# A fused cross-attention and FFN kernel on one core: new orders of the setup's steps, of four early slots on GpSimd, of one batch's tiles and of N's high and low parts

## The chip, the core and the metric

The kernel runs on one core of a Trainium2 chip. The metric is the device time of one launch in microseconds. Three runs of the kernel before took 2051.66 us (median), from 2050.03 to 2053.55.

The engines are called PE or TensorE (matmuls), DVE or VectorE, ACT or ScalarE, POOL or GpSimd, and SP (it issues all transfers). Each engine takes its own list of instructions strictly in order and meets the others through semaphores: a wait in the middle of a list holds everything behind it on that engine.

## The reference

```
x = x + xattn(ctx, layernorm(x), fside, fside, ln1, ln2, Wq, Wkv, Wout)   # q scaled and shifted per head
x = x + tanh(layernorm(x) @ W.T @ aux1 @ aux2 + bias)

xattn:  ln = layernorm(latents);  kn = layernorm(context)
        q  = ln @ Wq (16 heads of 64);  k, v = kn @ Wkv
        q  = q * (1 + scale) + shift
        out = softmax(q k / 8) v;  out @ Wout
```

x is 16 batches of 1024 rows of 512; the context has 64 rows in each batch. All is float32 at full accuracy, so every operand of a product is split into a high and a low part and each product is made of three matmuls (high by high, high by low, low by high).

## The kernel before, in words

**What is precomputed.** The three FFN matrices are multiplied into one, W3. For each batch the queries never appear: M (512 x 1024) is Wq times that batch's keys, so that the scores of a tile of 128 rows are x M, and N (1024 x 512) is that batch's values times Wout, so that the attention's output is p N.

**The setup** (`setup_sp`, `setup_pool`, `setup_act`, `setup_dve`, `setup_pe`, to about 133 us) loads 22 chunks of weights through a ring of five buffers, and eight tiles of context through three. Each engine runs a list of steps. The step `split c` of a chunk is ACT's high part (L419, or L411 and L415 where the columns are centred), then a low part by DVE (L476, L471) or, for the chunks in `POOL_LO`, by POOL (L373); SP loads chunk c + 5 into the buffer once chunk c is split. `stats i` and `norm i` (L449 to L453, POOL's pow at L367, L458, L462) normalise context tile i. `turn i` is its four transposes (PE L590), ACT's high part (L424) and DVE's low part (L482) in N_hi and N_lo, which serve as buffers here. `kv n` (32 of them, four buffers in PSUM) is one product of context and weights: sixteen of v (n under 16; ACT copies it out at L428), sixteen of k (DVE scales it twice in `k_scale`, L525 and L527), stored by SP at L312 from two buffers `kv_out`. `kb` sums the bias (PE L534, L535; ACT's copy at L385; SP's store at L287). Products kv 0 to 7 need turns 0 to 3, and kv 8 to 15 need turns 4 to 7 with their low parts. PE's order stands in `pe_steps`; before, SP, ACT, DVE and POOL share one list behind their front lists, `later_steps`, made from `beside`.

**Then M of batches 0 and 1** is made in 16 steps (`fold_m_pe`, L757 to L759; `m0_act` L768, `m0_dve` L783, and the copies of batch 1's part at L763 into eight buffers `m1_raw`, which SP stores at L347). The first four buffers lie in `stage_more`, the next two in two x buffers, the last two in the buffer S of the scores.

**The slots.** 128 tiles of rows go through a pipeline, one tile a slot: slot t computes the scores of tile t (PE, 24 matmuls), the product p N of tile t-2 (24), W3 of tile t-4 (12). m is t mod 8; a batch has eight tiles. For a tile, DVE adds the bias to the scores (L1319) and takes maxima (L1324), POOL subtracts them (L1458), ACT takes exp (L1222), DVE sums (L1330, L1333), POOL normalises (L1465), SP writes p and reads it back rearranged (L1067, L1084), DVE turns it (L1341), ACT and DVE make its high and low parts pT_hi and pT_lo (L1227, L1350). The next tile's xT_hi and xT_lo are ACT's and POOL's (L1020, L1025).

**N of the next batch** is made in the slots with m = 1 from the second batch on (t = 9, 17, ..., 121): `fold_n_pe` makes eight products of three matmuls at the slot's end (bank<-Wo_hi,bdv). Four banks hold them, so product p from the fifth on waits for the low part of product p-4:

```python
                if p < len(use):
                    free(p)
                else:
                    pe.wait_ge(s_nl, b8 + p - len(use) + 1)
```

ACT copies each to N_hi (L981), DVE subtracts for N_lo (L987). In `slot_act` and `slot_dve` this stands at the slot's end, behind the first half of the previous tile's p:

```python
            if tile_of(t - 1):
                pT_hi_part(0, t - 1)
            ...
            if m == 1 and 1 < t < T:
                fold_n_act(act, t - 1, range(8))
```

The next slot's scores wait for the fifth and sixth low part, since they use the same banks.

**M of the batches from 2 on** is made beside the slots in 128 small tiles (`tile_pe`, L877 to L880), four places A to D in a slot, given by `tile_at`: batches 2 and 3 (32 tiles of two batches, where DVE adds two halves, L891) in slots 2 to 9, four in each; batches 4 to 7 in slots 10 to 25, two in each; batches 8 to 15 in slots 26 to 89, one in each. Even ones of the first 32 use bank 2, which the fold of N uses too. They are stored, and loaded again a batch ahead as `land` (L942), split by ACT (L957) and POOL (L961).

Of the kernel before, what the change touches and what calls it, by code (L numbers as in the profile page):

```python
# [1587 lines left out]
```

## Time and profile before

| | |
|---|---|
| median of three runs | 2051.66 us (2050.03 to 2053.55) |
| the profiled execution | 2051.34 us, of which the span from first to last instruction is 2049.5 |
| PE busy | 2027.4 us of the span, 99% |
| DVE, ACT, POOL busy | 1520.5, 1319.4, 1349.7 us |
| mean granted TensorE clock | 0.999 |
| DMA | 431.54 MB, 210 GB/s of it to and from HBM |

A row of a timeline gives the start in us from the span's start, how long it lasted, the engine, the line, the operation, output<-inputs, shapes and the number of instructions merged; in brackets, how long the engine was idle before it and what ended that. Matmuls overlap in the pipeline: one of 512 columns is shown 0.39 us long, but in a full stream they start 0.227 apart. DMA issues (SPq) are times of the queue, not of the transfer.

### The profile page before, as it was taken

How to read it: one execution, taken by the hardware profiler on the slowest of the kernel's cores; microseconds unless marked ns; L12 is line 12 of the kernel's file. 1: busy time of each engine (PE TensorE's matmuls, PEld its weight loads, DVE VectorE, ACT ScalarE, POOL GpSimd, SP SyncE). 2: the span in 40 equal slices, each digit the busy share in tenths (PEclk: the TensorE clock that was granted, in tenths of full speed). 3: DMA queues.
4: the chain of work that ended last, by engine and by line, in shares of the span. 5: the costliest groups of instructions: out<-in, count | busy, mean ns of one | idle time of the engine just before them, and what ended most of it. 6: DMA issues, size and time to landing. Idle time of an engine off the chain costs nothing.

```text
span 2049.5 us, 31380 instructions
## 1 busy us (share of the span) xinstructions
PE 2027.4 (99%) x9180; PEld 1681.4 (82%) x9180; DVE 1520.5 (74%) x2414; ACT 1319.4 (64%) x3005; POOL 1349.7 (66%) x1466
## 2 busy tenths in 40 slices
PE   9999999999999999999999999999999999999998
PEld 7777878888888888888888888888888888888887
DVE  7567777776777777777777777777777777787776
ACT  4455667666766666666666667666666666666654
POOL 3136766766676776767676776767677676767564
PEclk9999999999999999999999999999999999999999
DMA  7657988878787887878788787878767576666653
GB/s 263 197 176 211 271 232 245 251 225 248 222 227 206 219 223 208 226 204 231 195 232 219 208 224 206 230 197 217 211 185 211 174 207 179 200 184 191 178 170 118
DMA packets 502490, 431.54 MB, mean 211 GB/s; under 512 B 54832, under 2 KB 408240, under 8 KB 502320
## 3 DMA queue, kind: packets, MB, share of 16 engines
q1 hardware_dynamic: 502320, 429.54, 74.6%
q8 instruction: 74, 1.21, 0.3%
q14 instruction: 96, 0.79, 0.1%
HBM read 251.33 MB, written 178.06 MB: 210 GB/s over the span
## 4 chain that ended last, share of the span: by engine, by line
PE 86%; DVE 3%; DMA 2%; ACT 2%; issue 2%; POOL 2%; SPq 2%; DVEq 0%; ACTq 0%; POOLq 0%
PE bank L161 34%; PE bank L1176 21%; PE bank L166 17%; PE bank L1179 10%; DMA m_scratch<-evac 1%; PE bank L880 1%; PE bank L879 1%; POOL area L1458 1%; POOL area L1465 1%; DVE N_lo L987 0%; DVE area L1319 0%; SPq L321 0%; DVE row_max L1324 0%; DVE turned L1341 0%; ACT bank L992 0%
## 5 line engine op out<-in xcount | busy, mean ns | idle before, releaser
L1458 POOL TENSOR_TENSOR area<-area,row_max 128x256 f32<-128x256 f32 x512 | 353.8, 712 | 145.8 <-DVE row_max L1324 145.8
L1176 PE MATMUL bank<-N_hi,pT_hi 128*128 128x512 f32 x1024 | 398.7, 389 | 2.6 <-DVE N_lo L987 1.3
L161 PE MATMUL bank<-M_hi,xT_hi 128*128 128x512 f32 x1024 | 398.7, 389 | 0.0
L161 PE MATMUL bank<-M_lo,xT_hi 128*128 128x512 f32 x1024 | 398.7, 389 | 0.0
L1176 PE MATMUL bank<-N_lo,pT_hi 128*128 128x512 f32 x1024 | 398.6, 389 | 0.0
L1227 ACT CAST pT_hi<-turned 128x512 fp32r<-128x512 f32 x256 | 159.1, 622 | 337.4 <-DVE turned L1341 337.4
L1465 POOL TENSOR_TENSOR area<-area,row_inv 128x512 f32<-128x512 f32 x256 | 269.2, 1052 | 114.7 <-DVE row_inv L1333 114.6
L1482 POOL TENSOR_TENSOR area<-area 128x512 f32<-128x512 f32 x127 | 165.4, 1303 | 239.3 <-ACT area L1266 239.3
L1330 DVE TENSOR_REDUCE row_sum<-area 128x8 f32<-128x512 f32 x256 | 174.4, 681 | 167.5 <-ACT area L1222 166.7
L1350 DVE TENSOR_TENSOR pT_lo<-turned,pT_hi 128x512 fp32r<-128x512 f32 x256 | 196.1, 766 | 119.2 <-ACT pT_hi L1227 119.2
L166 PE MATMUL bank<-M_hi,xT_lo 128*128 128x512 f32 x1024 | 273.9, 389 | 0.8 <-POOL xT_lo L1025 0.7
L1179 PE MATMUL bank<-N_hi,pT_lo 128*128 128x512 f32 x1024 | 273.7, 389 | 0.0
L1222 ACT ACTIVATE area<-area 128x512 f32<-128x512 f32 x256 | 160.2, 626 | 127.8 <-POOL area L1458 127.1
L1176 PEld LDWEIGHTS bank<-N_hi,pT_hi 128*128 128x128 f32 x1024 | 192.2, 188 | 42.3 <-DVE N_lo L987 1.5
L166 PEld LDWEIGHTS bank<-M_hi,xT_lo 128*128 128x128 f32 x1024 | 192.1, 188 | 41.4 <-POOL xT_lo L1025 1.7
L1179 PEld LDWEIGHTS bank<-N_hi,pT_lo 128*128 128x128 f32 x1024 | 192.2, 188 | 39.9
L1176 PEld LDWEIGHTS bank<-N_lo,pT_hi 128*128 128x128 f32 x1024 | 192.3, 188 | 39.5
L161 PEld LDWEIGHTS bank<-M_lo,xT_hi 128*128 128x128 f32 x1024 | 192.3, 188 | 39.4
L161 PEld LDWEIGHTS bank<-M_hi,xT_hi 128*128 128x128 f32 x1024 | 192.3, 188 | 39.4 <-ACT xT_hi L1020 0.2
L1319 DVE SCALAR_TENSOR_TENSOR area<-bank,rs,area 128x512 f32<-128x512 f32 x256 | 187.1, 731 | 19.7 <-PE bank L166 15.9
L161 PE MATMUL bank<-W_lo,x2T_hi 128*128 128x512 f32 (+1 forms) x512 | 199.3, 390 | 0.0
L161 PE MATMUL bank<-W_hi,x2T_hi 128*128 128x512 f32 (+1 forms) x512 | 199.0, 389 | 0.0
(183 smaller groups left out, 3923.3 us busy)
## 6 DMA issues: line engine op xcount, KB each, us to landing
p_scratch<-area SPq DMA_DIRECT2D x256, 256.0 KB, 2.6
p_moved<-p_scratch SPq DMA_DIRECT2D x512, 128.0 KB, 4.3
area<-x_dram SPq DMA_DIRECT2D x128, 256.0 KB, 4.5
area<-x_turned_dram SPq DMA_DIRECT2D x128, 256.0 KB, 4.0
x_scratch<-area SPq DMA_DIRECT2D x127, 256.0 KB, 3.0
x_moved<-x_scratch SPq DMA_DIRECT2D x508, 64.0 KB, 3.5
y_dram<-area SPq DMA_DIRECT2D x127, 256.0 KB, 3.6
land<-m_scratch SPq DMA_DIRECT2D x120, 256.0 KB, 2.8
```

What stands on the lines that cost most here:

```text
L161: mm = eng.matmul(ps, sh, mv, start=(n == 0), stop=False)
L166: mm = eng.matmul(ps, sl, mh, start=False, stop=(k == len(pairs) - 1))
L1176: pe.matmul(O_ps[:], st(pT_hi, k), n_cols(mv, k), start=(k == 0 and mv is N_hi), stop=False)
L1179: mm = pe.matmul(O_ps[:], st(pT_lo, k), n_cols(N_hi, k), start=False, stop=(k == 7))
L1222: act.activation(s, s, ACT.Exp).then_inc(s_ex[q], 1)
L1227: act.copy(half_of(pT_hi, q), turned[:]).then_inc(s_pTh[q], 1)
L1319: dve.scalar_tensor_tensor(out=half_of(S[t % 2], q), in0=S_ps[q][:], scalar=rs1[:, 0:1], in1=half_of(bias, q), op0=ALU.mult, op1=ALU.add). ...
L1330: dve.tensor_reduce(row_sum[t % 2][:, hs], heads(half_of(S[t % 2], q)), AX_XY, ALU.add).then_inc(s_sum[q], 1)
L1350: dve.tensor_tensor(half_of(pT_lo, q), turned[:], half_of(pT_hi, q).bitcast(F32), ALU.subtract).then_inc(s_pTl[q], 1)
L1458: last = pool.tensor_tensor(s, s, row.to_broadcast([P, 2, 4, J2]), ALU.subtract)
L1465: pool.tensor_tensor(s, s, inv, ALU.mult).then_inc(s_p[q], 1)
L1482: pool.tensor_tensor(xr[u % RING], xr[u % RING], hid, ALU.add).then_inc(s_y, 1)
```

## The change

1. The setup's shared list is cut into one for each engine. PE takes turn 3 ahead of the last part of W3, and turns 4 to 7 behind kv 2, 4, 5, 6 (before: 1, 3, 4, 5). DVE makes W3's low parts in the order 2, 3, 0, 1, with context tile 4's norm between, and takes stats, norm and turn of tiles 5 to 7 in a new order. ACT takes turns 4 to 7 behind kv 3, 5, 6, 7 (before 2, 4, 5, 6). The low parts of chunks 11 and 13 go from DVE to POOL. SP loads chunks 15 to 18 behind kv 2, 4, 6, 8 (before 0, 1, 4, 7), and context tile 7 behind kv 3 (before 1).
2. DVE's low parts of the four Wout chunks move one step later than ACT's high parts, and its k0 steps too. SP's first loads of x go from step 29 to 27.
3. The first high part of x moves from ACT to POOL.
4. M of batch 1 is staged first in S, then in the x buffers, then in `stage_more`; who needs S or the x buffers waits for the first four stores alone.
5. Slots 0 and 3 on POOL: the first subtraction goes ahead of xT_lo in slot 0, and xT_lo ahead of the two normalisations in slot 3.
6. The last four tiles of two batches go from slot 9 to slot 10, and all later tiles one slot on.
7. In the slots with m = 1, ACT makes N_hi 0 and 1 before pT_hi, and 2 to 7 after it. DVE makes N_lo 0 and 1 before the turn of p, N_lo 2 between the turn and pT_lo, and 3 to 7 after it.

```diff
-        m1_raw = [stage_more[...] for i in range(4)] + xr[2:4] + [S[0][...] for i in range(2)]
+        M1_EARLY = 4
+        m1_raw = [S[0][...] for i in range(2)] + xr[2:4] + [stage_more[...] for i in range(4)]
...
-                    ("w3_hi", 2), ("w3_lo", 2), ("turn", 2), ("w3_hi", 3), ("w3_lo", 3), ("turn", 3)]
+                    ("w3_hi", 2), ("w3_lo", 2), ("turn", 2), ("w3_hi", 3), ("turn", 3), ("w3_lo", 3)]
+        W3_LO = (2, 3, 0, 1)
...
-            some("turn", 2, 3) + some("split", 7, 8) + some("w3", 0, 1, 2, 3) + [("stats", 4), ("norm", 4)]
-        pool_front = some("stats", 0, 1) + some("split", 6) + some("stats", 2, 3) + some("split", 9) + some("stats", 4)
-        beside = {0: [("split", 10), ("stats", 5), ("norm", 5)], 1: [("split", 11), ("load", 7), ("stats", 6), ("norm", 6)],
-                  2: [("turn", 4), ("stats", 7), ("norm", 7)], 4: [("turn", 5), ("split", 12)],
-                  5: [("turn", 6)], 6: [("turn", 7)], 7: [("split", 13)],
-                  24: [("k0_load", 0)], 26: [("k0", 0)], 27: [("k0", 1)], 29: [("x0", 0)]}
+            some("turn", 2, 3) + some("split", 7, 8) + some("w3", *W3_LO[:2]) + [("stats", 4), ("norm", 4)] + some("w3", *W3_LO[2:]) + \
+            [("stats", 5), ("norm", 5), ("turn", 4), ("split", 10), ("stats", 6), ("norm", 6), ("turn", 5), ("stats", 7), ("norm", 7)] + \
+            some("turn", 6) + some("split", 12) + some("turn", 7)
+        pool_front = some("stats", 0, 1) + some("split", 6) + some("stats", 2, 3) + some("split", 9) + some("stats", 4, 5, 6) + \
+            some("split", 11) + some("stats", 7) + some("split", 13)
+        beside_sp = {2: some("split", 10), 3: some("load", 7), 4: some("split", 11), 6: some("split", 12), 8: some("split", 13),
+                     24: [("k0_load", 0)], 27: [("x0", 0)]}
+        beside_act = {0: some("split", 10), 1: some("split", 11), 3: some("turn", 4), 4: some("split", 12), 5: some("turn", 5),
+                      6: some("turn", 6), 7: some("turn", 7) + some("split", 13), 26: [("k0", 0)], 27: [("k0", 1)]}
+        beside_dve = {27: [("k0", 0)], 28: [("k0", 1)]}
...
-            beside[(20, 22, 25, 28)[g]] = [("split", WQ_FIRST + 4 + g)]
+            beside_act[(20, 22, 25, 28)[g]] = some("split", WQ_FIRST + 4 + g)
+            beside_dve[(21, 23, 26, 29)[g]] = some("split", WQ_FIRST + 4 + g)
...
-            pe_steps += [("kv", n)] + ([("turn", {1: 4, 3: 5, 4: 6, 5: 7}[n])] if n in (1, 3, 4, 5) else [])
+            pe_steps += [("kv", n)] + ([("turn", {2: 4, 4: 5, 5: 6, 6: 7}[n])] if n in (2, 4, 5, 6) else [])
...
-        POOL_LO = (6, 9)
+        POOL_LO = (6, 9, 11, 13)
...
-                tile_at[2 + m, place] = 4 * m + i
+                tile_at[2 + m + m // (TPB - 1), place] = 4 * m + i
...
             if n == 2:
                 pe.wait_ge(s_nl, 8)
+            if n == 28:
+                pe.wait_ge(s_nl, 8 + 7)
...
                 if t == 0 and q == 0:
-                    dve.wait_ge(s_m1w, 16 * 8)
+                    dve.wait_ge(s_m1a, 16 * M1_EARLY)
...
             evacuate("C")
+            folds = m == 1 and 1 < t < T
+            if folds:
+                fold_n_act(act, t - 1, range(2))
             if tile_of(t - 1):
                 pT_hi_part(0, t - 1)
...
-            if m == 1 and 1 < t < T:
-                fold_n_act(act, t - 1, range(8))
+            if folds:
+                fold_n_act(act, t - 1, range(2, 8))
...
             sum_tile("C")
+            folds = m == 1 and 1 < t < T
+            if folds:
+                fold_n_dve(dve, t - 1, range(2))
             if tile_of(t - 1):
                 ...
                 turn_p(0, t - 1)
                 ...
+                if folds:
+                    fold_n_dve(dve, t - 1, range(2, 3))
                 pT_lo_part(0, t - 1)
             if m == 0 and 0 < t < T:
                 diag_lo(dve, bdv, s_vh, s_vp, t // TPB)
-            if m == 1 and 1 < t < T:
-                fold_n_dve(dve, t - 1, range(8))
+            if folds:
+                fold_n_dve(dve, t - 1, range(3, 8))
```

## Rows read from the trace of the kernel before

**Rows 1.** The page: busy time by engine, and the granted clock in 40 slices.
```profile
PE 2027.4 (99%) x9180; PEld 1681.4 (82%) x9180; DVE 1520.5 (74%) x2414; ACT 1319.4 (64%) x3005; POOL 1349.7 (66%) x1466
...
PEclk9999999999999999999999999999999999999999
```
**Rows 2.** The timeline of TensorE: the warm-up, kv 8, and the idle times.
```profile
1.52 4.86 PE L540 MATMUL bank<-bdk 128*128 128x512 f32 x12 [1.52 <-POOL bdk L360]
...
40.59 0.63 PE L590 MATMUL bank<-evac,area 128*128 128x128 f32 x4 [1.49 <-DVE area L462]
...
59.89 0.39 PE L161 MATMUL bank<-N_hi,Wo_hi 128*128 128x512 f32 x1
...
126.50 0.47 PE L534 MATMUL bank<-x2T_hi,bdv 128*128 128x512 f32 x1 [0.50 <-ACT area L385]
...
143.83 0.36 PE L757 MATMUL bank<-bdk,M_hi 128*128 128x256 f32 x1 [2.49 <-DVE stage_more L763]
...
173.22 0.47 PE L1176 MATMUL bank<-N_hi,pT_hi 128*128 128x512 f32 x1 [1.26 <-ACT pT_hi L1227]
...
196.14 1.20 PE L166 MATMUL bank<-M_hi,xT_lo 128*128 128x512 f32 x4 [0.75 <-POOL xT_lo L1025]
...
280.46 0.47 PE L877 MATMUL bank<-k_parts 128*128 128x256 f32 x2 [1.09 <-DVE evac L891]
...
285.74 0.50 PE L161 MATMUL bank<-Wo_hi,bdv 128*128 128x512 f32 x1 [0.69 <-DVE evac L891]
...
288.47 0.50 PE L161 MATMUL bank<-Wo_hi,bdv 128*128 128x512 f32 x1 [1.07 <-DVE N_lo L987]
...
533.59 0.50 PE L161 MATMUL bank<-Wo_hi,bdv 128*128 128x512 f32 x1 [0.55 <-DVE N_lo L987]
```
**Rows 3.** Timelines of DVE, ACT and TensorE: the fold of N in slot 33.
```profile
647.50 0.63 DVE L1431 TENSOR_TENSOR area<-bank,area 128x512 f32<-128x512 f32 x1
648.05 0.70 DVE L1341 STREAM_TRANSPOSE turned<-p_moved 128x512 f32<-128x512 f32 x1
...
651.25 5.45 DVE L987 TENSOR_TENSOR N_lo<-bank,N_hi 128x512 fp32r<-128x512 f32 x8 [0.73 <-ACT N_hi L981]
...
648.83 0.62 ACT L1227 CAST pT_hi<-turned 128x512 fp32r<-128x512 f32 x1 [1.04 <-DVE turned L1341]
650.63 5.35 ACT L981 CAST N_hi<-bank 128x512 fp32r<-128x512 f32 x8 [1.18 <-PE bank L166]
...
649.75 0.39 PE L161 MATMUL bank<-Wo_hi,bdv 128*128 128x512 f32 x1
```
**Rows 4.** The timeline of ACT in slot 25: N_hi right behind pT_hi.
```profile
531.25 0.62 ACT L1227 CAST pT_hi<-turned 128x512 fp32r<-128x512 f32 x1 [1.26 <-DVE turned L1341]
531.78 2.04 ACT L981 CAST N_hi<-bank 128x512 fp32r<-128x512 f32 x4
```
**Rows 5.** The timeline of DVE in slot 97, a slot without tiles of M.
```profile
1593.34 5.28 DVE L987 TENSOR_TENSOR N_lo<-bank,N_hi 128x512 fp32r<-128x512 f32 x8
```
**Rows 6.** Timelines of DVE, ACT and SP in the setup, 29 to 61 us.
```profile
29.34 0.75 DVE L462 SCALAR_TENSOR_TENSOR area<-area,rs 128x512 f32<-128x512 f32 x1 [0.52 <-POOL rs L367]
...
41.49 0.69 DVE L449 BATCH_NORM_STATS2 area<-area 128x6 f32<-128x512 f32 x1
...
43.76 0.75 DVE L462 SCALAR_TENSOR_TENSOR area<-area,rs 128x512 f32<-128x512 f32 x1 [0.52 <-POOL rs L367]
...
60.69 0.59 ACT L428 COPY area<-bank 128x512 f32<-128x512 f32 x1 [2.24 <-DMA kv_scratch<-area]
...
55.57 0.38 SPq L273 DMA_DIRECT2D area<-wqT_dram  x1
56.00 5.62 SPq L312 DMA_DIRECT2D kv_scratch<-area  x3
```
**Rows 7.** Timelines of ACT and DVE: two waits for stores, in M's steps and slot 0.
```profile
142.04 0.59 ACT L385 COPY area<-bank 128x512 f32<-128x512 f32 x1 [3.33 <-DMA bias_scratch<-area]
...
154.92 0.75 DVE L1319 SCALAR_TENSOR_TENSOR area<-bank,rs,area 128x512 f32<-128x512 f32 x1 [2.39 <-DMA m_scratch<-area]
```

More of the change, by code:

```diff
@@ L173, in build @@
         RING_W = 5
-        m1_raw = [stage_more[:, i * BANK:(i + 1) * BANK] for i in range(4)] + xr[2:4] + [S[0][:, i * BANK:(i + 1) * BANK] for i in range(2)]
+        M1_EARLY = 4
+        m1_raw = [S[0][:, i * BANK:(i + 1) * BANK] for i in range(2)] + xr[2:4] + [stage_more[:, i * BANK:(i + 1) * BANK] for i in range(4)]
         stage = stage + [stage_more[:, i * 2 * D:(i + 1) * 2 * D] for i in range(2)]
@@ L199, in build @@
         pe_steps = [("mix", 0), ("mix", 1), ("turn", 0), ("turn", 1), ("w3_hi", 0), ("w3_hi", 1), ("w3_lo", 0), ("w3_lo", 1),
-                    ("w3_hi", 2), ("w3_lo", 2), ("turn", 2), ("w3_hi", 3), ("w3_lo", 3), ("turn", 3)]
+                    ("w3_hi", 2), ("w3_lo", 2), ("turn", 2), ("w3_hi", 3), ("turn", 3), ("w3_lo", 3)]
+        W3_LO = (2, 3, 0, 1)
         some = lambda step, *tiles: [(step, i) for i in tiles]
         sp_front = some("split", 0, 1, 2, 3, 4, 5) + some("load", 3, 4) + some("w3", 0) + some("split", 6) + some("load", 5) + \
-            some("split", 7, 8, 9) + some("load", 6)
+            some("split", 7) + some("load", 6) + some("split", 8, 9)
@@ new lines, in build @@
+        beside_dve = {27: [("k0", 0)], 28: [("k0", 1)]}
+        for g in range(4):
+            beside_dve[(9, 10, 12, 14)[g]] = some("fold", g)
+            beside_act[11 + 2 * g] = some("split", WQ_FIRST + g)
+            beside_dve[11 + 2 * g] = some("split", WQ_FIRST + g)
+            beside_sp[11 + 2 * g] = some("split", WQ_FIRST + g)
+            beside_act[(20, 22, 25, 28)[g]] = some("split", WQ_FIRST + 4 + g)
+            beside_dve[(21, 23, 26, 29)[g]] = some("split", WQ_FIRST + 4 + g)
@@ L226, in build @@
             pe_steps += [("kb", n - 19)] if 19 <= n < 31 else []
-            later_steps += [("kv", n)] + beside.get(n, [])
+            sp_later += [("kv", n)] + beside_sp.get(n, [])
+            act_later += [("kv", n)] + beside_act.get(n, [])
+            dve_later += [("kv", n)] + beside_dve.get(n, [])
+        pool_later = [("kv", n) for n in range(4 * PAIRS)]
         kv_where = lambda n: (1 - n // 16, (n // 8) % 2, n % 8)
@@ L295, in setup_sp @@
             sp.dma_start(ident, ident_in).then_inc(s_ident, 16)
-            for step, i in sp_front + later_steps:
+            for step, i in sp_front + sp_later:
                 if step == "split" and i + RING_W < CHUNKS:
@@ L362, in setup_pool @@
             pool.wait_ge(s_const, 3)
-            for step, i in pool_front + later_steps:
+            for step, i in pool_front + pool_later:
                 if step == "stats":
@@ L392, in setup_act @@
         def setup_act(act):
-            for step, i in act_front + later_steps:
+            for step, i in act_front + act_later:
                 if step == "split":
@@ L444, in setup_dve @@
                 dve.memset(bdv[own, own].bitcast(F32), 1.0).then_inc(s_ones, 1)
-            for step, i in dve_front + later_steps:
+            for step, i in dve_front + dve_later:
                 if step == "stats":
@@ L1500, in slot_pool @@
                 land_lo(pool, 1)
-                xT_split_lo(pool, 3)
+            if t in (2, 3):
+                xT_split_lo(pool, t + 1)
             if t < T:
```

57 lines of the change are left out of this document (29 added, 28 removed).

## The prediction

> **What bounds the kernel now.** I read the totals first. TensorE is busy for 2027.4 of the 2049.5 us of the span, at the full clock in every slice of the page [rows 1]. So nothing another engine does faster there can pay, and a wait that a new order puts in front of TensorE costs its whole length: no idle time is there to swallow it. Then I read TensorE's timeline for its idle times. Nearly all lie before 290 us, with one at 533.59 [rows 2]. A matmul of 512 columns is shown 0.39 long but the next starts 0.227 later, so an idle time of x costs x + 0.16. With that, the waits the change aims at are worth: 40.59 (a norm is late) 1.65, 126.50 0.66, 143.83 2.65, 173.22 1.42, 196.14 0.91, the three of slot 9 (280.46, 285.74, 288.47) 1.25 + 0.85 + 1.23 = 3.33, 533.59 (slot 25) 0.71. Together 11.3 us, 0.55%: the most that it can win.
>
> **N ahead of the turn: 15 slots.** This part runs in every slot with m = 1 (t = 9, 17, ..., 121), though only slots 9 and 25 have a wait there. In slot 33 [rows 3] the fold's first product starts at 649.75; call that F. Each product is three matmuls, 0.68. ACT reads the first at F+0.88 (650.63), DVE makes its low part at F+1.50 (651.25), after 0.73 idle, and all eight follow at 0.68 each, done at F+6.95. What did DVE do before? At 648.05, 0.55 after its sum of L1431 began, it turned p, and it made pT_lo while TensorE was still in W3 and in the first product: the turn cost nothing.
>
> In the new order DVE stands still from 648.1 until N_hi 0 is there. N_lo 0 and 1 end at F+2.18 and F+2.87, as before. Then the turn, F+2.8 to F+3.5. ACT's pT_hi waits for it (0.78 from turn to copy, 648.05 to 648.83): F+3.6. ACT's N_hi 2 is queued behind pT_hi, 0.53 later (531.25 to 531.78 [rows 4]): F+4.11. DVE's N_lo 2 comes 0.62 after that, F+4.73 to F+5.41, then pT_lo to F+6.0, and N_lo 3 to F+6.62. In the old order those two were done at F+3.55 and F+4.23.
>
> TensorE's product p, from 4 on, uses the bank of p-4 and waits for N_lo of p-4. Products 4 and 5 (due F+2.72, F+3.40) don't wait. Product 6, due F+4.08, waits until F+5.46: 1.38. Product 7, due then at F+6.14, waits until F+6.67: 0.53. The fold ends 1.91 later, and TensorE goes on with the next slot's scores, which need N_lo 4 (F+7.2, before product 7 ends at F+7.35). In the late slots (97 to 121, without tiles) DVE makes the eight without idle time ahead of them [rows 5], since pT_lo runs right up to them; in the new order it has nothing left to do there before N_hi 0, so it is ready as early as in slot 33: the same 1.91.
>
> Bounds: 1.4 if N_lo 3 followed closely enough for product 7 to wait for nothing, 2.3 if each of the two restarts costs some 0.1 more and DVE is late by a tenth. I take 1.91: it is made of the rows themselves. Thirteen slots (all but 9 and 25): 13 x 1.91 = +24.8. Slot 25: +1.91 - 0.71 = +1.20. Slot 9: its tiles go to slot 10, so its 3.33 goes and 1.91 comes: -1.42. Together **+24.6**.
>
> **Tiles in slot 10.** The same instructions move; TensorE's sum is unchanged. Slot 10 follows the folds, so its scores (24 matmuls, 5.4) and DVE's backlog come first; tile A waits for N_lo 6, due F+8.6, and would start at F+12.8. On SP, tile 31's store and later tile 63's now go out in the slot in which the next land load waits for them. Between them are queued four moves of x2 and y's store, and the load waits for GpSimd's land_lo anyway; p's write is behind it. Priced at nothing; if that cover is gone, one landing time twice, some 3 us each at most.
>
> **Setup, up to product kv 8 (59.89 [rows 2]).** Turn 3 goes ahead of the last w3_lo: its norm ends at 30.1 (29.34 + 0.75 [rows 6]) and it starts 0.68 sooner, and with it N_lo and product kv 0 (32.99 to 32.3). Turn 4 now comes after kv 2, due 41.0; its norm, that 0.68 and two low parts (1.2) sooner than 40.4, is there at 38.6. The 1.65 of 40.59 goes. Now the DVE list: norm 5, *turn 4*, split 10, norm 6, *turn 5*, norm 7. ACT makes turn 4's high part only after kv 3, and its copies of kv 2 and 3 wait for kv_out to be stored: with kv 0's store 0.68 sooner and kv 1's not behind chunk 15 any more, these two copies are made at 44.2 and 44.9, and turn 4's high part from 45.4 to 46.0. DVE, free at 42.7 (38.6, two low parts, a norm), stands until 46.0; low parts of turn 4 and split 10 to 47.8; a norm takes 3.02 (41.49 to 44.51 [rows 6]), norm 6 ends at 50.8. TensorE wants it at 49.8: +1.0. SP can load chunk 15 only at 47.8, with kv 3's store behind it. In the old run a store queued behind a chunk (55.57, 56.00) let ACT go on at 60.69, 4.6 later [rows 6]. So ACT copies kv 5 at 52.9, turn 5's high part ends at 54.0, its low part at 54.7, norm 7 at 57.7. TensorE wants that at 54.0: +3.7. Last, turn 7's high part now stands behind kv 7's copy on ACT, and kv 8 needs its low part: 0.2 + 0.5 + 0.6 + 0.7 + 0.1 = 2.1 after kv 7 ends. With 0.36 for turn 7 and 2.72 for kv 7, kv 8 starts at 62.85 instead of 59.89: **+2.96**. Bounds: +0.8 if no store held ACT, +4.5 if the landings take a microsecond and a half more. I take the walk, as its landing has a row. The low parts 11 and 13 on GpSimd stand ahead of pow 7 and of SP's chunk 16; both are ready before norm 7 asks, so nothing.
>
> **Setup, the rest.** DVE now scales k before it waits for ACT's WO and k0 parts: -0.66 (126.50). SP's five loads of step x0 go out after kv 27 instead of between kv 29 and kv 30, so the bias stores behind them land in time: ACT's idle time of 3.33 [rows 7] goes, and TensorE's 2.65 with it. x's first high part leaves ACT for GpSimd, off the path. Slot 0's first read of the scores waits for four stores of M instead of eight: DVE's 2.39 [rows 7] goes, p of tile 0 is earlier, and the 1.42 at 173.22 goes. In slot 3 xT_lo is ahead of the two normalisations: -0.91 (196.14), paid for by p about 1.5 later, which has 4 us of room before its pT. Sum: 2.96 - 0.66 - 2.65 - 1.42 - 0.91 = **-2.7**. Bounds -7 and +1.
>
> **Sum.** 24.6 - 2.7 = +21.9 on the profiled execution's own 2051.34, which is 0.3 under the median of 2051.66: 2073.
>
> **Rivals.**
> *A, the order of N costs nothing* (the copies find room that I don't see, or products 6 and 7 aren't on the path). Then 15 x 1.91 falls away: 2073 - 28.7 = 2044.6, faster. For it: slots 9 and 25 do show products waiting for N_lo 0, which this order cures. Against it: the cure is worth 0.71 and 1.23, in two slots of 15, and DVE and ACT take their lists in order. 0.10.
> *B, only part of it bites*: product 7's wait is hidden and DVE finds the turn's place cheaper, 0.7 to 1.0 a slot: 15 x 0.85 less 4.0 less 2.7 gives 2057. 0.09. It would still be slower.
> *C, the clock falls.* In the old trace 2.49 us of idle left it at the full level. The wait for norm 7 would be 3.7. If TensorE then ran a dozen matmuls at 1.2 GHz, as its first twelve did (4.86 us for 12 [rows 2], against 2.9 at full clock), that is +2: 2075. 0.15, out of the forecast's share, and inside its range. The Trainium skill (TensorE: Matmul & The Clock Gate, HAM oscillation) has waits for data put the array back to half clock; no idle time of this trace is as long as the one walked here.
> *D, the change doesn't do what it says*: stats and folds have conditions of their own (m = 1, t > 1), and these hold for 15 slots. 0.01.
>
> **How the numbers follow.** A measurement of this kernel tells 0.2% (4 us) from no change. The forecast with C has 0.80 and runs from 15 x 1.4 - 4.0 - 7 = +10 to 15 x 2.3 - 4.0 + 1 = +31.5: 2061 to 2083. I set the range at 2056 to 2082, which takes in B's middle and leaves A out. Slower 0.89, same 0.02, faster 0.09.
>
> **What the profile would show.** Right: every m = 1 slot has two idle times of TensorE at a fold's matmul, released by DVE's N_lo at L987's place, 1.4 and 0.4 to 0.5; DVE idle some 3 us before N_lo 0; TensorE's busy share down to 98% in all slices; kv 8 near 62 to 63, no idle time of 2.5 near 140, none at 280. Wrong: fold products 227 ns apart through slot 33, or DVE turning p before the fold's first high part.

## The result, and the profile after

The changed kernel takes 2079.14 us (median of 4 runs, 2076.0 to 2080.15), the kernel before 2050.87 in the same series: 1.0133 times as long, with a 95% interval of [1.0118, 1.0148]. That is 28.3 us more. The forecast was 21.9 more, 2073, with a range that ended at 2082: slower, as forecast, and 6 us more so. The profiled execution took 2079.4 with a span of 2077.6, 28.1 more than the span of before.

TensorE's sum on the page went up by 11.0, its instructions are as many as before, and every slice is still shown at the full clock:

```profile
PE 2038.4 (98%) x9180; PEld 1681.3 (81%) x9180; DVE 1518.7 (73%) x2412; ACT 1313.1 (63%) x3004; POOL 1343.7 (65%) x1469
...
PEclk9999999999999999999999999999999999999999
```

The idle time of TensorE went up by the other 17.1. Neither sum alone is the loss, since a matmul that no other overlaps is shown longer. The measure used from here on is the **excess**: the distance from one matmul's start to the next's, less the 0.227 that 512 columns take undisturbed (0.114 for 256, 0.080 for 128), wherever it is over 0.03. It holds the idle time, the slow restart behind it, and the time that matmuls lose at half clock. Added up over TensorE's timeline it gives, for the two kernels and two runs of the next section:

| stretch, us | before | after | run 1 (N undone) | run 4 (N and kv order undone) |
|---|---|---|---|---|
| 0 to 64, to kv 8 | 8.9 | 12.6 | 12.5 | 7.6 |
| 64 to 135 | 2.6 | 4.1 | 3.3 | 1.4 |
| 135 to 200, M's steps, slots 0 to 3 | 7.6 | 2.1 | 2.1 | 2.1 |
| 200 to 300, slots 4 to 9 | 3.8 | 4.6 | 4.9 | 3.8 |
| 300 to 545, slots 10 to 25 | 0.8 | 4.0 | 2.1 | 0.8 |
| 545 to the end | 0.1 | 24.2 | 0.1 | 0.1 |
| sum | 23.9 | 51.5 | 24.9 | 15.8 |

The difference of the sums, 27.6, is all but 0.5 of the 28.1 of the spans. 24.1 of it lies in the last row. Each column is one execution. Three entries hold time at half clock from 64 us on: 1.5 of the 4.1 of the changed kernel, 1.6 of run 1's 3.3, and 1.5 of run 1's 4.9 from 200 to 300.

**The fold of slot 33**, which answers to [rows 3]. TensorE's timeline of the changed kernel:

```profile
656.67 0.39 PE L166 MATMUL bank<-Wo_hi,bdv 128*128 128x512 f32 x1
658.28 0.50 PE L161 MATMUL bank<-Wo_hi,bdv 128*128 128x512 f32 x1 [1.22 <-DVE N_lo L1004]
658.62 0.39 PE L161 MATMUL bank<-Wo_lo,bdv 128*128 128x512 f32 x1
658.85 0.40 PE L166 MATMUL bank<-Wo_hi,bdv 128*128 128x512 f32 x1
659.48 0.50 PE L161 MATMUL bank<-Wo_hi,bdv 128*128 128x512 f32 x1 [0.24 <-DVE N_lo L1004]
659.82 0.39 PE L161 MATMUL bank<-Wo_lo,bdv 128*128 128x512 f32 x1
```

DVE's timeline there:

```profile
654.32 1.38 DVE L1004 TENSOR_TENSOR N_lo<-bank,N_hi 128x512 fp32r<-128x512 f32 x2 [3.12 <-ACT N_hi L998]
655.61 0.70 DVE L1361 STREAM_TRANSPOSE turned<-p_moved 128x512 f32<-128x512 f32 x1
657.54 0.69 DVE L1004 TENSOR_TENSOR N_lo<-bank,N_hi 128x512 fp32r<-128x512 f32 x1 [1.23 <-ACT N_hi L998]
658.15 0.68 DVE L1370 TENSOR_TENSOR pT_lo<-turned,pT_hi 128x512 fp32r<-128x512 f32 x1
658.75 3.08 DVE L1004 TENSOR_TENSOR N_lo<-bank,N_hi 128x512 fp32r<-128x512 f32 x5
```

And ACT's:

```profile
656.40 0.62 ACT L1244 CAST pT_hi<-turned 128x512 fp32r<-128x512 f32 x1 [1.43 <-DVE turned L1361]
656.93 2.04 ACT L998 CAST N_hi<-bank 128x512 fp32r<-128x512 f32 x4
```

The row of 5.45 us that DVE made without a break in [rows 3] is cut in three, with 3.12 idle ahead of it (in the old order the turn and pT_lo lay in that time) and 1.23 in the middle. TensorE stands at products 6 and 7: 1.38 + 0.11 at the first (the matmul behind the one that waited starts 0.34 after it instead of 0.227), 0.40 + 0.11 at the second, 2.0 in all. All 15 folds show the pair, the first at 288.97, the last at 1965.87.

**The setup.** TensorE's timeline of the changed kernel has the two new waits that were walked (before turn 6 and before kv 8), and two more further on that were not: 105.39 is 1.16 long where the same matmul waited 0.47 in the kernel before (at 99.51), and 115.92 is new. Those of [rows 2] at 40.59, 126.50, 143.83, 196.14, 280.46 and 285.74 are gone:

```profile
53.27 1.05 PE L606 MATMUL bank<-evac,area 128*128 128x128 f32 x4 [2.15 <-DVE area L478]
...
54.54 0.63 PE L161 MATMUL bank<-N_lo,Wo_hi 128*128 128x512 f32 x1
54.96 0.63 PE L161 MATMUL bank<-N_hi,Wo_hi 128*128 128x512 f32 x1
...
63.35 0.63 PE L161 MATMUL bank<-N_hi,Wo_hi 128*128 128x512 f32 x1 [1.89 <-DVE N_lo L498]
63.78 0.63 PE L161 MATMUL bank<-N_lo,Wo_hi 128*128 128x512 f32 x1
...
105.39 0.47 PE L550 MATMUL bank<-x2T_hi,bdv 128*128 128x512 f32 x1 [1.16 <-ACT area L401]
...
115.92 0.47 PE L550 MATMUL bank<-x2T_lo,bdv 128*128 128x512 f32 x1 [0.56 <-ACT area L401]
```

The matmuls behind 53.27 and behind 63.35 start 0.43 apart, twice the usual distance: the granted clock was at its lower level, 1.2 GHz (0.50 from 54 to 56 and from 64 to 66 us), for a time too short for the page's slices to show it. DVE's norm 6, which 53.27 waited for, is long: its second step took 2.77 where that of the next norm took 0.75.

```profile
50.35 2.77 DVE L478 SCALAR_TENSOR_TENSOR area<-area,rs 128x512 f32<-128x512 f32 x1 [0.51 <-POOL rs L380]
...
57.10 0.75 DVE L478 SCALAR_TENSOR_TENSOR area<-area,rs 128x512 f32<-128x512 f32 x1 [0.51 <-POOL rs L380]
```

What GpSimd did in that time:

```profile
50.22 2.35 POOL L386 TENSOR_TENSOR M_lo<-area,M_hi 128x1024 fp32r<-128x1024 f32 x1
```

### The profile page after: what moved, and what is told of

It reads as the page before. It is cut to its first block, busy times and chain, and to the rows that moved or that the text cites. A ratio compares the mean times of both kernels' runs of the same rounds, so it can differ in the third digit from the quotient of the medians.

```text
span 2077.6 us, 31382 instructions
## 1 busy us (share of the span) xinstructions
PE 2038.4 (98%) x9180; PEld 1681.3 (81%) x9180; DVE 1518.7 (73%) x2412; ACT 1313.1 (63%) x3004; POOL 1343.7 (65%) x1469
## 4 chain that ended last, share of the span: by engine, by line
PE 86%; DVE 3%; ACT 2%; issue 2%; POOL 1%; DMA 1%; SPq 0%; DVEq 0%; ACTq 0%; POOLq 0%
PE bank L161 34%; PE bank L1193 22%; PE bank L166 17%; PE bank L1196 11%; PE bank L896 1%; PE bank L895 1%; DVE N_lo L1004 1%; DVE turned L1361 1%; ACT N_hi L998 1%; DVE pT_lo L1370 1%; ACT pT_hi L1244 1%; POOL area L1483 0%; DMA m_scratch<-evac 0%; PE bank L775 0%; PE bank L773 0%
```

## The experiments

Each run has its own comparison with the kernel before, on the same chip (medians of before 2050.95 to 2051.44). Runs 1 to 4, 5 to 8, 9 to 11 and 12 were on different chips.

**Is it N's order? Run 1** takes the new order of N out of the changed kernel, **run 2** puts it alone into the kernel before. Run 2's edit (run 1's is its reverse, in the changed kernel):

```diff
+    fold_n_act(act, t - 1, range(2))
     pT_hi_part(0, t - 1)
-    fold_n_act(act, t - 1, range(8))
+    fold_n_act(act, t - 1, range(2, 8))
...
+    fold_n_dve(dve, t - 1, range(2))
     turn_p(0, t - 1)
+    fold_n_dve(dve, t - 1, range(2, 3))
     pT_lo_part(0, t - 1)
-    fold_n_dve(dve, t - 1, range(8))
+    fold_n_dve(dve, t - 1, range(3, 8))
```

> The changed kernel with one part undone: in slots with m = 1 ACT and DVE make all eight parts of N after the turn of p, as in the kernel before; setup, tiles in slot 10 and the rest stay changed. My theory (each of the 15 folds lost 1.38 + 0.11 + 0.40 + 0.11 = 2.0 us by start-to-start distances of the matmuls, slots 9 and 25 included): 15 x 2.0 = 30 comes back less the 0.7 that slot 25 then waits again, 2079.1 - 29.3 = 2049.8, and no idle time of TensorE at the fold of slot 33 or later. Rival (the two idle times of each fold only stand in for a wait that comes anyway, for instance for N_lo 4 at the next scores): the time stays above 2070.

> The kernel before with the new order of N alone (two parts ahead of the turn of p, a third ahead of its low part, in every slot with m = 1). My theory: 15 folds lose 2.0 us each, slot 25's 0.7 goes, and in slot 9, which still has its tiles here, the old waits of 0.85 and 1.23 are replaced by the new pair: 2050.9 + 30 - 0.7 - 2 = 2078. Rival (the loss in the changed kernel comes from the tiles having moved to slot 10 or from slot 0 to 3's orders, and not from N): within 5 us of 2051.

Run 1: 2050.97, ratio 0.9997 [0.9988, 1.0006]. Run 2: 2079.39, ratio 1.0138 [1.0124, 1.0151]. N's order alone costs 28.4 us on the kernel before, and its removal gives back 28.2. In run 1 no fold from slot 33 on waits. But slots 9 and 25 do, although the tiles have left slot 9:

```profile
285.72 0.50 PE L161 MATMUL bank<-Wo_hi,bdv 128*128 128x512 f32 x1 [1.93 <-DVE N_lo L1004]
```

Those waits, 3.9 in slots 9, 17 and 25, are as long as those of [rows 2] (4.0). All the rest of the change together (setup, slots, tiles) is worth nothing, 0.0 with a bound of about 2 us each way, where the prediction's terms gave -6.

**Where does the fold's wait come from? Runs 5, 6 and 8** are the changed kernel with other cuts of N's row. Run 5 moves one copy of ACT; run 6 puts N_hi 2 and 3 ahead of pT_hi and N_lo 2 and 3 ahead of pT_lo; run 8 has all eight parts ahead of the turn.

```diff
 run 5, on ACT
-    fold_n_act(act, t - 1, range(2))
+    fold_n_act(act, t - 1, range(3))
     pT_hi_part(0, t - 1)
     ...
-    fold_n_act(act, t - 1, range(2, 8))
+    fold_n_act(act, t - 1, range(3, 8))
 run 6, so too on ACT with 4, and on DVE
     turn_p(0, t - 1)
-    fold_n_dve(dve, t - 1, range(2, 3))
+    fold_n_dve(dve, t - 1, range(2, 4))
     pT_lo_part(0, t - 1)
     ...
-    fold_n_dve(dve, t - 1, range(3, 8))
+    fold_n_dve(dve, t - 1, range(4, 8))
 run 8, on DVE, and so too on ACT ahead of pT_hi
-    fold_n_dve(dve, t - 1, range(2))
+    fold_n_dve(dve, t - 1, range(8))
     turn_p(0, t - 1)
     ...
-    fold_n_dve(dve, t - 1, range(2, 3))
     pT_lo_part(0, t - 1)
     ...
-    fold_n_dve(dve, t - 1, range(3, 8))
```

> The changed kernel, with ACT making N_hi 2 ahead of pT_hi instead of behind it in the 15 slots with m = 1; VectorE's order unchanged. My theory of the wait (product 6 waits for N_lo 2, which waits for N_hi 2, which stands behind pT_hi on ACT, which waits for the turn): N_lo 2 then follows the turn at once and ends at F + 4.2, product 6 (due F + 4.08) waits about 0.15 instead of 1.22 idle; pT_lo and N_lo 3 follow N_hi 3, which is still behind pT_hi, so N_lo 3 ends at F + 5.6 and product 7 waits about 0.7 instead of 0.23. Each fold loses 1.0 instead of 2.0: 2079.1 - 15 = 2064. Rival (what costs is the turn's own 0.7 and pT_lo's 0.6 on VectorE, wherever ACT's parts stand): product 6 still waits over 0.9, total within 3 us of 2079.

> The changed kernel with N_hi 2 and 3 ahead of pT_hi on ACT, and N_lo 2 and 3 ahead of pT_lo on VectorE (the turn still behind N_lo 1). My theory: only the turn's 0.7 lies between the parts of N until product 7 has its bank; product 6 waits 0.15, product 7 nothing, and the next scores at most 0.45 for N_lo 4, which comes behind pT_lo: 0.3 to 0.7 a fold, 2079.1 - 15 x 1.5 = 2057 (2054 to 2060). Rival as for the run before: no better than it, 2064 or more.

> The changed kernel with all eight parts of N (ACT and DVE) ahead of the turn of p in the 15 slots with m = 1, nothing between them. Theory A (the loss comes from cutting N's row in two, not from putting N first; pT has room, since p x N starts at F + 10.9 and pT_lo would be there at F + 9.1): no idle time in any fold, slots 9 and 25 included, nothing new at p x N, and 2079.1 - 15 x 2.0 = 2049, a little under the run with N's order undone (2051.0) because that one still waits 2.1, 0.3 and 1.5 in slots 9, 17 and 25: 2046 to 2048. Theory B (the turn is then late: the second turn, x2's turn and the softmax behind it on VectorE are each put off by 1.3, and p x N or the scores' readers wait): 0.5 to 2 us a slot again, 2055 to 2075.

Run 5: 2062.04, ratio 1.0054 [1.0041, 1.0068]. One copy moved by one place on ACT gives back 17 of the 28 us. Its fold of slot 33, on DVE's timeline:

```profile
652.26 0.70 DVE L1361 STREAM_TRANSPOSE turned<-p_moved 128x512 f32<-128x512 f32 x1
652.89 0.65 DVE L1004 TENSOR_TENSOR N_lo<-bank,N_hi 128x512 fp32r<-128x512 f32 x1
```

N_lo 2 follows the turn at once, 0.63 behind its start instead of 1.93. Product 6 has no idle time left; product 7's has grown:

```profile
655.12 0.50 PE L161 MATMUL bank<-Wo_hi,bdv 128*128 128x512 f32 x1 [0.57 <-DVE N_lo L1004]
```

The excess is 1.0 a fold. Run 6: 2054.13, ratio 1.0019 [1.001, 1.0028], 0.15 to 0.6 a fold from slot 17 on; what is left lies mostly at the next scores, which wait for N_lo 4. So most of the wait was the chain turn, pT_hi, N_hi 2, and not the 0.7 of the turn itself.

Run 8: 2062.26, ratio 1.0052 [1.0039, 1.0064]. Theory A falls, B holds: no fold waits, but the wait is somewhere else. TensorE in the slot after 33:

```profile
672.04 1.20 PE L166 MATMUL bank<-M_hi,xT_lo 128*128 128x512 f32 x4 [0.35 <-POOL xT_lo L1042]
```

and GpSimd ahead of it:

```profile
669.69 1.05 POOL L1484 TENSOR_TENSOR area<-area,row_inv 128x512 f32<-128x512 f32 x1 [0.89 <-DVE row_inv L1351]
670.70 1.28 POOL L1042 TENSOR_TENSOR xT_lo<-area,xT_hi 128x512 fp32r<-128x512 f32 x1
```

The turn that now comes behind N puts off all that follows on DVE: the second reciprocal comes at F + 19.2 instead of F + 16.9 in the kernel before (F is the start of the fold's first product, as in the prediction), GpSimd's normalisation waits for it, and x's low part stands behind that in GpSimd's list. 13 such waits after 545 us come to 9.3 us; 5 us more lie between 300 and 520, most of them at M's tiles, which wait for a copy of ACT (1.24, 1.07 and 0.94 idle at 390.71, 441.28 and 471.71). Theory A gave pT its room (F + 9.1 against F + 10.9) and did not follow what stands behind pT.

**Run 4** is the changed kernel with N's order undone, as in run 1. Besides, it takes back the orders between kv 0 and kv 8: splits 10 to 13 and turns 4 to 7 stand in the places of before on SP, ACT, DVE and GpSimd. On TensorE this holds for turns 5 and 6 alone. Turns 4 and 7 stay behind kv 2 and 6, as in the changed kernel (before: 1 and 5), where the expectation below says "PE as before". The rest of the change is kept. The edit, without N's part:

```diff
-    [("stats", 5), ("norm", 5), ("turn", 4), ("split", 10), ("stats", 6), ("norm", 6), ("turn", 5), ("stats", 7), ("norm", 7)] + \
-    some("turn", 6) + some("split", 12) + some("turn", 7)
+    [("split", 10), ("stats", 5), ("norm", 5), ("split", 11), ("stats", 6), ("norm", 6), ("turn", 4), ("stats", 7), ("norm", 7)] + \
+    some("turn", 5) + some("split", 12) + some("turn", 6, 7) + some("split", 13)
...
-    beside_act = {0: some("split", 10), 1: some("split", 11), 3: some("turn", 4), 4: some("split", 12), 5: some("turn", 5),
+    beside_act = {0: some("split", 10), 1: some("split", 11), 2: some("turn", 4), 4: some("turn", 5) + some("split", 12),
...
-    pe_steps += [("kv", n)] + ([("turn", {2: 4, 4: 5, 5: 6, 6: 7}[n])] if n in (2, 4, 5, 6) else [])
+    pe_steps += [("kv", n)] + ([("turn", {2: 4, 3: 5, 4: 6, 6: 7}[n])] if n in (2, 3, 4, 6) else [])
...
-    POOL_LO = (6, 9, 11, 13)
+    POOL_LO = (6, 9)
```

> The changed kernel with two parts undone: the order of N, and the orders of the setup between product kv 0 and kv 8 (places of split 10 to 13 and turn 4 to 7 on SP, ACT, DVE, GpSimd and PE as before). What stays of the change: turn 3 ahead of the last w3_lo, the later WO and k0 parts, step x0 loaded after kv 27, the high part of x on GpSimd, slots 0 and 3, tiles in slot 10. My theory: the stay-behinds are worth what I priced, 0.7 + 2.65 + 1.4 + 0.9, and the three waits of slot 9 are 3.3 less: about 2050.9 - 8 = 2043, with kv 8 started at 59.2 to 59.9. Rival (those gains are taken back by the new waits that the changed kernel shows at 105, 116, 178, 211, 226 and 231 us): 2047 to 2050.

2045.40, ratio 0.9976 [0.9966, 0.9985], faster than both kernels, by less than the 8 us that I expected. TensorE's only wait between kv 3 and kv 8 is now

```profile
49.30 0.63 PE L605 MATMUL bank<-evac,area 128*128 128x128 f32 x4 [0.52 <-DVE area L477]
```

and kv 8 starts at 58.44 instead of 63.35. The orders up to kv 8 therefore cost the changed kernel 5.6 us against those of run 4 (2050.97 less 2045.40). That is not to be held against the 2.96 of the walk, which was from the kernel before: run 4's kv 8 also starts 1.45 ahead of the old 59.89. TensorE's waits of before for turn 4 (1.49 idle at 40.59) and for turn 7 (0.88 at 53.95) are not there, and these two turns are the ones that stay later in TensorE's list. No run takes their places back alone.

**Which of them? Run 3** returns the low parts of chunks 11 and 13 from GpSimd to DVE, **run 9** takes run 1 and puts turn 7 ahead of kv 7's copy on ACT and of split 12 on DVE.

```diff
 run 3
-    some("turn", 6) + some("split", 12) + some("turn", 7)
+    some("split", 11) + some("turn", 6) + some("split", 12) + some("turn", 7) + some("split", 13)
...
-    POOL_LO = (6, 9, 11, 13)
+    POOL_LO = (6, 9)
 run 9
-    some("turn", 6) + some("split", 12) + some("turn", 7)
+    some("turn", 6, 7) + some("split", 12)
...
-    6: some("turn", 6), 7: some("turn", 7) + some("split", 13)
+    6: some("turn", 6, 7), 7: some("split", 13)
```

> The changed kernel with one part undone: the low parts of chunks 11 and 13 are made by VectorE again instead of GpSimd (11 ahead of turn 6, 13 behind turn 7). Theory A (GpSimd's low part, 2.35 to 2.54 us, held VectorE's instructions beside it: the second step of norm 6 took 2.77 instead of 0.75, and the stall of TensorE that this made longer put its clock down): norm 6's second step is 0.75 to 0.8 again, TensorE's idle time ahead of turn 6 falls from 2.15 to 1.0 or less, the clock stays at its full level there, and the kernel is 2 to 5 us faster than the changed one: 2074 to 2077. Theory B (VectorE has no room, its two extra low parts of 0.62 each delay norm 7 as much as they free norm 6): within 1 us of 2079.1.

> The changed kernel with N's order undone (as in the first run, 2051.0) and with turn 7 ahead of the copy of kv 7 on ACT and ahead of split 12 on VectorE. My theory: the 1.89 us for which TensorE stands ahead of product kv 8 are turn 7's high part behind kv 7's copy and nothing else; with both moved, turn 7's low part is there at about 60.7, before kv 7 ends at 61.5, so kv 8 starts 1.9 sooner, and, with no idle time there, the clock keeps its full level behind it, which is worth up to 1.7 more: 2047 to 2049. Rival (ACT's wait for kv 5's store at 53 and the clock that fell at 53.3 set kv 8): within 0.7 us of 2051.0.

Run 3: 2081.77, ratio 1.0148 [1.0134, 1.0162]: 2.6 slower than the changed kernel, where theory A wanted 2 to 5 faster. The two intervals overlap, and the traces bear the difference out. Theory A's readings were right and its verdict wrong. Without GpSimd's low part beside it the norm is short again:

```profile
50.43 0.75 DVE L477 SCALAR_TENSOR_TENSOR area<-area,rs 128x512 f32<-128x512 f32 x1 [0.51 <-POOL rs L379]
```

and turn 6 waits 0.13 at 51.33. But norm 7 ends at 58.1 all the same, since DVE waits for ACT (3.31 ahead of 54.49) and ACT for a store, so turn 7 stands for what turn 6 no longer does. And SP's load of chunk 16 now waits for a low part of DVE that is behind norm 7:

```profile
49.70 0.50 SPq L324 DMA_DIRECT2D kv_scratch<-area  x1
59.27 0.38 SPq L285 DMA_DIRECT2D area<-wqT_dram  x1
59.70 1.79 SPq L324 DMA_DIRECT2D kv_scratch<-area  x2
```

with two stores behind the load, and ACT behind the stores:

```profile
64.56 0.58 ACT L443 COPY area<-bank 128x512 f32<-128x512 f32 x1 [8.73 <-DMA kv_scratch<-area]
```

kv 8 starts at 66.41, 3.1 later. In the changed kernel that load goes out at 52.64, behind GpSimd's low part. So GpSimd's low part of chunk 11, which the prediction had put at nothing, is worth its price here, for SP's sake.

Run 9: 2048.48, ratio 0.9986 [0.9977, 0.9995], 2.5 faster than run 1. The two intervals overlap, but the trace shows where the time went. TensorE goes from kv 7 into kv 8 without a gap, at the full clock:

```profile
60.08 1.07 PE L166 MATMUL bank<-N_hi,Wo_lo 128*128 128x512 f32 x4
60.98 0.39 PE L161 MATMUL bank<-N_hi,Wo_hi 128*128 128x512 f32 x1
61.21 0.39 PE L161 MATMUL bank<-N_lo,Wo_hi 128*128 128x512 f32 x1
```

In run 9 the clock also fell behind turn 6, and that cost kv 8 next to nothing: where it stayed up (runs 5 and 6), TensorE waited 1.5 and 1.4 for norm 7 instead.

**What took away the wait at 143.83? Run 10** is run 4 with SP's step x0 back behind kv 29; **run 12** is run 10 with, besides, DVE's second low parts of WO and of k0 ahead of the scaling of k again.

```diff
 run 10
-    27: [("x0", 0)]
+    29: [("x0", 0)]
 run 12, besides
-    beside_dve = {27: [("k0", 0)], 28: [("k0", 1)]}
+    beside_dve = {26: [("k0", 0)], 27: [("k0", 1)]}
...
-    beside_dve[(21, 23, 26, 29)[g]] = some("split", WQ_FIRST + 4 + g)
+    beside_dve[(20, 22, 25, 28)[g]] = some("split", WQ_FIRST + 4 + g)
```

> The kernel of the fourth run (2045.4) with SP's step x0 back behind kv 29, as in the kernel before. My theory: the bias stores land late again, ACT waits for them, and TensorE has an idle time of about 2.5 at the first products of the folding of M (143.83 in the kernel before; 2.65 with the pitch): 2048. Rival (that wait went away because kv 8 comes sooner or because x's first high part left ACT): under 0.7 us of 2045.4, no idle time over 1 us between 125 and 150.

> The kernel of the run before last but one (x0 back behind kv 29, 2044.2, without the idle time that I had put down to x0's place), in which VectorE also makes the second low parts of WO and k0 ahead of the scaling of k again, as in the kernel before. Theory A (SP reaches x0 and the last bias stores late because kv 29's scaled rows are late, and these are late because VectorE's scaling stands behind a low part that waits for ACT: 131.50 in the kernel before, 1.9 ahead of the first product of the folding of M, and 125.12, 5.2 ahead of it, in the run without the idle time): SP's loads of x0 are pushed to the first product of the folding again, ACT's copy of a bias sum waits 2 to 3.3 us for its store, TensorE stands 1.5 to 2.5 there, and 0.7 comes back before it: 2044.2 + 2.4 to 3.3 = 2047. Theory B (x's first high part, moved from ACT to GpSimd, or the places of split 10 to 13 were what freed it): under 0.7 us of 2044.2 and no idle time over 1 us between 125 and 150.

Run 10: 2044.17, ratio 0.9970 [0.9958, 0.9981], and no idle time there: the new place of x0 is not needed. Run 12: 2048.24, ratio 0.9982 [0.9973, 0.9992], 4.1 more, and the wait is back. The two intervals just overlap; by the traces the excess from 69 to 160 us is 4.0 more, 1.9 of it at this wait and 2.1 at bias sums ahead of it. On DVE's timeline of run 12 kv 29's two scalings stand behind the low part that waits for ACT:

```profile
127.98 1.48 DVE L491 TENSOR_TENSOR Wo_lo<-area,Wo_hi 128x1024 fp32r<-128x1024 f32 x1 [1.04 <-ACT Wo_hi L434]
129.38 0.68 DVE L540 TENSOR_TENSOR area<-bank,evac 128x512 f32<-128x512 f32 x1
129.98 0.68 DVE L542 TENSOR_TENSOR area<-bank,evac 128x512 f32<-128x512 f32 x1
```

ACT's wait for a bias store and TensorE's behind it, which answer to [rows 7] and [rows 2]:

```profile
139.65 0.59 ACT L400 COPY area<-bank 128x512 f32<-128x512 f32 x1 [2.46 <-DMA bias_scratch<-area]
```

```profile
141.44 0.36 PE L772 MATMUL bank<-bdk,M_hi 128*128 128x256 f32 x1 [1.62 <-DVE area L778]
```

So DVE's order alone takes the wait away where x0 is late. Whether x0's early place alone would have done it too is not shown: no run has x0 early and DVE's order as before.

**The tiles and slot 9. Run 11** is run 4 with the tiles back in slots 9, 17 and so on. **Run 7** is run 4 with all eight parts of N ahead of the turn in slots 9, 17 and 25 alone.

```diff
 run 11
-    tile_at[2 + m + m // (TPB - 1), place] = 4 * m + i
+    tile_at[2 + m, place] = 4 * m + i
...
-    tile_at[TPB + 3 + m, "C"], tile_at[TPB + 3 + m, "D"] = 32 + 2 * m, 32 + 2 * m + 1
+    tile_at[TPB + 2 + m, "C"], tile_at[TPB + 2 + m, "D"] = 32 + 2 * m, 32 + 2 * m + 1
...
 run 7, on ACT, and so too on DVE ahead of the turn
+    early = t in (9, 17, 25)
+    if early:
+        fold_n_act(act, t - 1, range(8))
     if tile_of(t - 1):
         pT_hi_part(0, t - 1)
     ...
-    if m == 1 and 1 < t < T:
+    if m == 1 and 1 < t < T and not early:
         fold_n_act(act, t - 1, range(8))
```

> The kernel of the fourth run (2045.4) with the tiles back in slots 9, 17 and so on, and the end of the first phase's tiles as before (no wait of tile 28 for N_lo 7). Theory A, as I forecast it: the tiles in slot 9 caused all its waits, 3.33 there instead of 0, and 0.7 in slot 25: 2045.4 + 3.3 = 2048.7. Theory B, from the trace of the fourth run (slot 9 without tiles still waits 2.57 at its fold): the waits of slot 9 become 3.3 instead of 2.6, + 0.7, not to be told from 2045.4.

> The kernel of the fourth run (order of N and setup up to kv 8 as before, 2045.4), with all eight parts of N ahead of the turn of p in slots 9, 17 and 25 alone, the slots in which VectorE still has arrears. Theory: the waits of 2.41 and 0.47 idle at the folds of slots 9 and 25 go (2.57 and 0.64 by start-to-start distance), nothing else moves: 2045.4 - 3 = 2042.4. Rival (in these slots the arrears are ahead of the turn and of N alike, so the fold waits as long for N_lo 0): within 0.7 us of 2045.4.

Run 11: 2043.80, ratio 0.9960 [0.9947, 0.9974]; theory B. It is the fastest of all, though its interval overlaps with those of runs 4 and 10, so that these three can't be ranked. Slot 9 loses 2.9 with the tiles and 2.7 without. Run 7: 2046.28, ratio 0.9974 [0.9964, 0.9984], no gain. Neither expectation held: the fold of slot 9 has no wait left, and TensorE stands later, in slots that the edit doesn't touch:

```profile
384.45 0.36 PE L894 MATMUL bank<-k_parts,wst 128*128 128x256 f32 x1 [1.22 <-ACT evac L923]
```

and at 434.72, 464.92 and 495.28, where run 4 has none. From 270 to 545 run 7 loses 5.1, run 4 3.4. Run 8 has waits of the same kind at 390.71, 441.28 and 471.71; what the two share is N ahead of the turn in slots 9, 17 and 25. Which list carries the arrears from slot 9 to slot 15 no run shows.

## Why the prediction was right, and where it missed

The sign and the mechanism of the main term were right, and the size was 6.4 us short by the medians (6.2 by the span of the profiled execution, 5.7 by the excess). The setup as a whole went the other way than forecast: by the excess up to 270 us it cost 1.5 instead of giving back 2.7. That was small beside the 26 us of N, so the forecast held; the measured time lies 3 us inside the upper end of its range.

*N's order, forecast +24.6, measured +28.4 alone on the kernel before.* The walk holds to a hundredth. In slot 33 N_lo 0 starts at 654.32, which is F + 1.50 with F = 652.82; then the turn is at F + 2.79 (forecast 2.8), pT_hi at 3.58 (3.6), N_hi 2 at 4.11 (4.11), N_lo 2 at 4.72 (4.73), product 6 at 5.46 (5.46), product 7 at 6.66 (6.67). The term was 1.91 and measured 2.0: left out was the slow restart behind product 7's wait, 0.11. 13 such folds give 26.1 instead of 24.8. Slot 25 has 2.0 for the old 0.8, +1.2 as forecast; slot 9 has 2.5 for 3.6, -1.2 where -1.42 was forecast. Together +26.1 in the changed kernel. Run 2's 28.4 is 2 more, which its interval (25 to 31) doesn't tell apart, and the clock fell once in its profiled execution.

*Tiles in slot 10, forecast 0 for the tiles and -3.33 for slot 9's old waits.* The step failed that put those waits down to the tiles. They stay without the tiles, at N_lo 0, which DVE reaches late behind the turn of p: from 270 to 300 run 4 loses 2.7 without the tiles and run 11 2.9 with them, and run 7, with N ahead of the turn there, has no wait at the fold. (Run 1 loses 3.8 there, of which 1.5 is half clock behind its wait.) In the changed kernel this was hidden, as N's new order has its 2.5 there in any case.

*Setup up to kv 8, forecast +2.96.* kv 8 started at 63.35 against a walk of 62.85, in the right order of waits: ACT's copy of kv 5 at 53.13 (52.9), norm 7 done at 57.85 (57.7), 2.05 ahead of kv 8 (2.1, and run 9 shows that it was turn 7's place). Two things were missed. One is DVE's norm 6, whose second step took 2.77 instead of 0.75 beside GpSimd's low part: "nothing" was written for low parts 11 and 13. TensorE waited 2.15 for turn 6, where the forecast had 1.0 and run 3, without GpSimd's low part, has 0.13. It cost kv 8 almost nothing, as norm 7 set the time: in run 3 norm 7 ends at 58.1 all the same, against 57.85. The Trainium skill (SBUF — State Buffer, Who interferes with whom) has VectorE and GpSimd share a port pair under an exclusive lock, where an operation of VectorE with two inputs in SBUF, issued second beside one of GpSimd that reads SBUF, stands until GpSimd's is over; by that rule, the trace agrees: GpSimd's ends at 52.57, DVE's at 53.12, 0.55 behind it. The same pair meets again at 63.59, where L508 takes 2.74 instead of 0.68. The other is the clock.

*Rival C, the clock, 0.15.* It happened: after 1.89 us idle at 63.35 the next eight distances are 0.43, 1.7 us more in all, as against the forecast's 2. Run 1, which has the same setup, had the same 1.89 idle at 63.26. It went on at 0.33 and 0.23, at full clock, and then fell too, some 1.2 us after the restart, for 1.6 us more in all:

```profile
64.06 0.39 PE L161 MATMUL bank<-N_lo,Wo_hi 128*128 128x512 f32 x1
64.29 0.43 PE L161 MATMUL bank<-N_hi,Wo_hi 128*128 128x512 f32 x1
64.52 0.62 PE L161 MATMUL bank<-N_lo,Wo_hi 128*128 128x512 f32 x1
64.94 0.63 PE L161 MATMUL bank<-N_hi,Wo_hi 128*128 128x512 f32 x1
```

In the profiled executions of runs 5 and 6, again with the same setup and the same 2.15 and 1.89 idle, it stayed at 2.4 GHz there. Run 5:

```profile
64.81 0.50 PE L161 MATMUL bank<-N_hi,Wo_hi 128*128 128x512 f32 x1 [1.89 <-DVE N_lo L498]
65.15 0.39 PE L161 MATMUL bank<-N_lo,Wo_hi 128*128 128x512 f32 x1
65.38 0.40 PE L161 MATMUL bank<-N_hi,Wo_hi 128*128 128x512 f32 x1
```

So it depends on the execution. The four executions of the changed kernel show a mean clock of 0.997, 0.998, 0.997 and 1.000, and the last is the one of 2076.0. In the kernel before 2.49 of idle (143.83) left the clock up; in run 2 the same wait, 2.25 long at 145.32, was followed by its fall 1.4 us after the restart, and in run 3, 3.53 (at 58.25) by its fall some 1 us after the restart. The Trainium skill (TensorE: Matmul & The Clock Gate, HAM oscillation) has waits for data put the array back to half clock; in that the trace agrees, with 1.89 and 2.15 us, though not in every execution.

*The rest of the setup, forecast -5.64 for four waits.* 143.83 (-2.65 forecast) went, -2.7. 173.22 and 196.14 (-1.42 and -0.91) brought -2.7 together, as the wait at 177.75 shrank too. At the bias sums 126.50 went as forecast (-0.66), but the wait of before at 99.51 grew by 0.7 (105.39) and 115.92 is new, so that from kv 8 to 135 us only 0.1 came back, half clock left out. Not forecast were 1.9 from 200 to 270, where three small waits for x's low part and a tile's operand are new; the last and longest of them (0.72 idle in the changed kernel) is between 0.2 and 1.5 in runs 1, 5 and 6, so this term is of one execution. And for the largest the prediction named one cause, "SP's five loads of step x0 go out after kv 27", where it had another at hand: runs 10 and 12 show that VectorE's scaling of k ahead of its wait for ACT removes it with x0 in the old place. That edit, priced at 0.66, is worth 4.1 when x0 is late (run 12 against run 10).

*The sums.* N 1.5, kv 8 0.5, the clock 1.7, the bias sums 0.6, 200 to 270 us 1.9, less 0.5 from 135 to 200: 5.7, which is what the forecast was short of the excess (27.6). The 0.5 by which the spans differ more is in none of these rows.

## What to carry to other kernels

A row of short copies that an engine makes in step with TensorE should not be cut by work whose result goes to another engine and comes back: it costs the round trip (here 1.93 instead of 0.63 between two parts), once for every repetition, and can only pay where the row is late. Follow each instruction that is put behind to its last reader, not to its first, since run 8's loss lay two engines further on. And a wait taken from a stretch in which the helping engines have arrears is not yet a gain: run 7's came back 100 us later.

## What the runs showed of the hardware

- One operation of VectorE with two inputs in SBUF took 2.77 instead of 0.75 beside a GpSimd operation of 2.35, and 2.74 instead of 0.68 beside one of 2.54: it stood for all of GpSimd's time, and did not share it.
- TensorE's clock fell to 1.2 GHz behind 1.89 and 2.15 us of idle in some executions, and stayed at 2.4 GHz behind the same two waits in others (runs 5 and 6) and behind 2.49 in the kernel before: the length of the idle time alone does not say whether it falls. It fell within 0.2 us of the restart at 53.27 and 63.35 in the changed kernel, and 1.1 to 1.4 us after it in runs 1, 2 and 3. It can come behind a fold's wait too: behind 1.93 at 285.72 in run 1, and it cost 1.5 there. This explains a part of the spread that the medians have to bear: run 1's ten executions lie between 2048.9 and 2054.0, and the three that a mean clock of 0.997 is shown for have 2051.1, 2052.4 and 2054.0. It is not all: twenty executions of the kernel before, with 0.998 to 1.000, lie between 2048.0 and 2055.9.
- Behind a wait of TensorE the second matmul of 512 columns starts 0.31 to 0.34 after the first instead of 0.23, at full clock: a wait costs 0.08 to 0.11 more than the idle time and the late first start show. At the folds it is 0.34.
